# Mixture-of-experts down-projection turned to tokens on the partitions, in a fused two-layer attention kernel

## The reference

```python
logits = jnp.einsum('bsd,de->bse', x, Wg)          # x: layer-normed, E = 8 experts
top_vals, top_idx = jax.lax.top_k(logits, 2)
probs = jax.nn.softmax(top_vals, axis=-1)
weights = jnp.einsum('bsk,bske->bse', probs, jax.nn.one_hot(top_idx, 8))
for e in range(8):
    u = jnp.einsum('bsd,dh->bsh', x, W1[e])        # D = 128, H = 256
    v = jnp.einsum('bsd,dh->bsh', x, W2[e])
    h = u * jax.nn.sigmoid(u) * v
    y = jnp.einsum('bsh,hd->bsd', h, W3[e])
    out = out + y * weights[..., e][..., None]
...
Q = (decoder_input @ W_q); K = (encoder_output @ W_k)   # next block, 16 heads of 8
```

## Time and profile before

| | |
|---|---|
| time, median of 3 runs | 232.7 us (232.6 to 235.12) |
| profiled execution, its own time | 232.4 us |
| its span, first to last instruction | 230.6 us |
| PE matmul busy | 191.9 us, 83% |
| PE weight load busy | 146.3 us, 63% |
| DVE busy | 167.3 us, 73% |
| ACT busy | 138.5 us, 60% |
| POOL busy | 121.5 us, 53% |
| mean granted TensorE clock | 0.947 of full |

### The profile page before, as it was taken

The page is one execution under the profiler, slowest core; times in us unless marked ns, Lnnn a source line. Parts: engine busy times, 40 slices in busy tenths (PEclk is TensorE's granted clock), DMA queues, the critical chain, the costliest instruction groups (busy, mean ns, idle before and its releaser), DMA issues.

```text
span 230.6 us, 4033 instructions
## 1 busy us (share of the span) xinstructions
PE 191.9 (83%) x1182; PEld 146.3 (63%) x1182; DVE 167.3 (73%) x408; ACT 138.5 (60%) x273; POOL 121.5 (53%) x140
## 2 busy tenths in 40 slices
PE   5858884887989999999989689799999999886320
PEld 4646772556767888788877477566867776654220
DVE  3775774187797787699764896798978978735664
ACT  2182845965535656456652569887968769573452
POOL 4368548994867998859991452222313222203512
PEclk9999998599999999999999889999999999999755
DMA  6990000001911420207400000000000000000002
GB/s 237 395 386 9 4 0 0 0 0 44 280 45 20 167 85 9 91 0 239 126 3 1 0 0 3 0 0 4 0 4 0 0 0 0 4 0 0 0 1 91
DMA packets 6292, 12.98 MB, mean 56 GB/s; under 512 B 1009, under 2 KB 1906, under 8 KB 6018
## 3 DMA queue, kind: packets, MB, share of 16 engines
q1 hardware_dynamic: 4688, 11.83, 15.1%
q10 hardware_dynamic: 1586, 0.93, 1.4%
HBM read 10.11 MB, written 0.56 MB: 46 GB/s over the span
## 4 chain that ended last, share of the span: by engine, by line
PE 54%; POOL 14%; DVE 13%; ACT 10%; issue 8%; DVEq 0%; POOLq 0%; ACTq 0%
POOL hids L308 7%; PE banks L1344 6%; PE bank L1325 6%; PE bank L1356 5%; PE bank L1097 4%; PE bank L1098 4%; PE bank L1099 4%; PE banks L1097 3%; PE banks L1099 3%; PE banks L1098 3%; POOL cpT L318 3%; PE bank L1111 2%; PE bank L1333 2%; PE bank L1271 2%; ACT raw L593 2%
## 5 line engine op out<-in xcount | busy, mean ns | idle before, releaser
L308 POOL TENSOR_TENSOR hids<-attT,hids 128x512 fp32r<-128x512 f32 x32 | 41.1, 1300 | 10.5 <-ACT hids L509 10.1
L965 DVE TENSOR_REDUCE negm<-bank 128x2 f32<-128x512 f32 x64 | 42.0, 687 | 5.3 <-PE bank L1325 4.0
L356 POOL TENSOR_TENSOR wx<-raw,const 32x256 fp32r<-32x256 f32 x32 | 19.5, 609 | 44.9 <-DVE raw L955 36.3
L593 ACT ACTIVATE raw<-banks 128x1024 f32<-128x1024 f32 x32 | 32.5, 1022 | 3.2 <-PE banks L1344 2.9
L509 ACT CAST hids<-attT 128x512 fp32r<-128x512 f32 x32 | 19.9, 621 | 18.8 <-DVE attT L886 10.7
L881 DVE SCALAR_TENSOR_TENSOR att<-att,bank 128x512 f32<-128x512 f32 x32 | 21.9, 684 | 12.5 <-ACT att L503 12.5
L1325 PE MATMUL bank<-wx 128*128 128x512 f32 x64 | 25.5, 440 | 1.6 <-DVE wx L975 1.5
L503 ACT ACTIVATE att<-bank 128x512 f32<-128x512 f32 x32 | 18.8, 595 | 9.4 <-PE banks L1099 7.7
L1097 PE MATMUL bank<-xT,wx 128*128 128x512 f32 x48 | 19.9, 415 | 0.8 <-DVE att L881 0.7
L1098 PE MATMUL bank<-xT,wx 128*128 128x512 f32 x48 | 19.2, 400 | 0.0
L1344 PE MATMUL banks<-wx 128*128 128x256 f32 x128 | 19.1, 293 | 0.0
(11 more groups left out here) (222 smaller groups left out, 462.9 us busy)
## 6 DMA issues: line engine op xcount, KB each, us to landing
rwb<-routing SPq DMA_DIRECT2D x8, 512.0 KB, 4.1
raw<-in_w SPq DMA_DIRECT2D x1, 2048.0 KB, 10.6
wx<-negm SPq DMA_DIRECT2D x1, 2048.0 KB, 8.7
raw<-in_w SPq DMA_DIRECT2D x1, 1024.0 KB, 10.1
xs<-in_x SPq DMA_DIRECT2D x2, 256.0 KB, 3.2
ctxT<-in_ctxT SPq DMA_DIRECT2D x1, 512.0 KB, 4.4
ctx<-in_ctx SPq DMA_DIRECT2D x1, 512.0 KB, 5.8
wl<-in_wl SPq DMA_DIRECT2D x1, 256.0 KB, 6.4
```

The source lines that it names most:

```text
L308: pool.tensor_tensor(hids[:, p, 1, k, :], hid[:, p, k, :], plain(hids[:, p, 0, k, :]), ALU.subtract).then_inc(S["hid_lo"], 1)
L593: act.activation(probs[:, g % 2, 2 * r:2 * r + 2, :, :].rearrange("p h k q -> p (h k q)"), pair[r][:, :], ACT.Exp, scale=ATT_SCALE).then_i ...
L965: dve.tensor_reduce(negm[:, g % 2, r // 2, c0:c0 + QUAD + 1:QUAD], bk[1 + r % 2][:, :].rearrange("p (h k) -> p h k", h=2), AX.X, ALU.max, ...
```

## The change

- `down` swaps its operands: `hids` is stationary, 128 tokens at a time, and W3 streams with 128 columns. Three products by two blocks by four token tiles make 24 matmuls instead of 6. The result has tokens on the partitions.
- `weigh` is four DVE instructions of 128 columns that multiply by `rw[:, tile, e]`, a value per partition, and add into `xs`. `accumulate`, the transposes of sum and weights, the store and broadcast of weights, and `add_experts` go.
- `gates` uses Silu instead of tanh, so `hidden` is one DVE instruction for a block instead of two. Two dummy activations put the loads of ACT's function table ahead of the first Silu and the next Exp. The router's softmax is a tanh.
- Routing is cut in `leaders` and the rest, a unit later. On PE `up(0)` goes ahead of `logits(0)`, and `up(1)` is issued in halves around `logits_turned(0)`.
- POOL makes the rest of `ctxTs` and `wqk` later; group 0 is projected ahead of `up(15)` and group 1 ahead of `down(14)`, into bank 7.

```diff
+            act.wait_ge(S["row_norm"], 1)
+            act.activation(spare[:, :], const[:, C_ZERO:C_ZERO + 1], ACT.Silu)
...
-                        act.wait_ge(S["gate_s"], HB * (n - 1) + k + 1)
-                    act.activation(tanhs[:, k, :], bk[2 * k][:, :], ACT.Tanh, scale=0.5).then_inc(S["tanh_s"], 1)
+                        act.wait_ge(S["hid_s"], HB * (n - 1) + k + 1)
+                    act.activation(silus[:, k, :], bk[2 * k][:, :], ACT.Silu).then_inc(S["silu_s"], 1)
...
+            for n in range(UNITS):
+                if n == 4:
+                    logits_out(1)
+                if n == UNITS - 1:
+                    proj_hi(0, 7)
+                gates(n, n == 0)
+                if n == 0:
+                    logits_out(0)
+                if n in (1, 5):
+                    gap_tanh(n // 5)
+                if n == UNITS - 1:
+                    act.wait_ge(S["km_zero"], 16)
+                    masked_keys(0, 0, True)
+                for k in range(HB):
+                    if n in (E + 3, E + 4):
+                        third_scaled(HB * (n - E - 3) + k)
+                    hidden_hi(n, k)
+                if n == UNITS - 3:
+                    norm_hi()
+            act.activation(spare[:, :], const[:, C_ZERO:C_ZERO + 1], ACT.Exp)
+            proj_hi(1, 7)
...
             def hidden(n):
...
-                    dve.scalar_tensor_tensor(gated[:, k, :], tanhs[:, k, :], 1.0, bk[2 * k][:, :],
-                                             ALU.add, ALU.mult).then_inc(S["gate_s"], 1)
-                    dve.wait_ge(S["gate_s"], HB * n + k + 1)
+                    dve.wait_ge(S["silu_s"], HB * n + k + 1)
...
-                    dve.tensor_tensor(hid[:, p, k, :], gated[:, k, :], bk[2 * k + 1][:, :], ALU.mult)\
+                    dve.tensor_tensor(hid[:, p, k, :], silus[:, k, :], bk[2 * k + 1][:, :], ALU.mult)\
...
             def weigh(n):
...
-                dve.tensor_tensor(out, bk[4 + n % 2][:, :], rwb[:, e, :], ALU.mult).then_inc(S["y_w"], 1)
+                dve.wait_ge(S["route_s"], 9 * (h + 1))
+                if e > 0:
+                    dve.wait_ge(S["y_w"], n)
+                for t in range(TPH):
+                    tile = h * TPH + t
+                    ins = dve.scalar_tensor_tensor(xs[:, tile, :], bk[4 + n % 2][:, t * P:(t + 1) * P],
+                                                   rw[:, tile, e:e + 1], xs[:, tile, :], ALU.mult, ALU.add)
+                ins.then_inc(S["y_w"], 1)
...
+            for n in range(UNITS):
+                if n == UNITS - 1:
+                    stack_keys(0, 0, True, 7)
+                    stack_queries(0, 0, True, 7)
+                hidden(n)
+                if n in (0, 4):
+                    leaders(n // 4)
+                if n in (1, 5):
+                    routing(n // 5)
...
+                if n >= 2:
+                    weigh(n - 2)
...
+            stack_keys(1, 1, True, 7)
+            stack_queries(1, 1, True, 7)
             weigh(UNITS - 2)
...
             maxima(0, 0, range(2), True)
-            stack_queries(1, 1, True)
-            stack_keys(1, 1, True)
+            weigh(UNITS - 1)
             maxima(0, 0, range(2, 4), True)
...
             def down(n):
...
-                for k in range(HB):
-                    ins = three(bk[4 + p][:, :], (w3[:, e, 0, k * P:(k + 1) * P], w3[:, e, 1, k * P:(k + 1) * P]),
-                                (hids[:, p, 0, k, :], hids[:, p, 1, k, :]), k == 0, k == HB - 1)
+                for t in range(TPH):
+                    rows = slice(t * P, (t + 1) * P)
+                    for k in range(HB):
+                        cols = slice(k * P, (k + 1) * P)
+                        pe.matmul(bk[4 + p][:, rows], hids[:, p, 0, k, rows], w3[:, e, 0, cols],
+                                  start=t == 0 and k == 0, stop=False)
+                        pe.matmul(bk[4 + p][:, rows], hids[:, p, 0, k, rows], w3[:, e, 1, cols], start=False, stop=False)
+                        ins = pe.matmul(bk[4 + p][:, rows], hids[:, p, 1, k, rows], w3[:, e, 0, cols],
+                                        start=False, stop=t == TPH - 1 and k == HB - 1)
...
+            up(0)
+            pe.wait_ge(S["v_ev"], 2)
+            logits(0)
+            up(1, (0,))
+            logits_turned(0)
+            up(1, (1,))
...
+                if n == UNITS - 1:
...
+                    for a in range(2):
+                        project(0, 0, 0, a, bank=7)
+                up(n)
+                if n == 4:
+                    logits_turned(1)
+                down(n - 2)
+                if n == 3:
+                    logits(1)
+                if n == UNITS - 3:
+                    turn("ln3", "x3T_ps", 6, 0)
+            for a in range(2):
+                project(1, 1, 0, a, bank=7)
             down(UNITS - 2)
...
+            pe.wait_ge(S["hid_s"], HB * UNITS)
             for r in range(2):
                 scores(0, 0, r, True)
+            down(UNITS - 1)
             for a in range(2):
-                project(1, 1, 0, a)
+                project(2, 2, 0, a)
```

More of the change, by code:

```diff
@@ L181, in build @@
               for i in range(8)]
+        leader = bk[7][:, 64:64 + TPH]
+        topf, shares = (bk[7][:, c0:c0 + 2 * TPH].rearrange("p (t r) -> p t r", r=2) for c0 in (72, 80))
+        second = bk[7][:, P:P + TPH * E].rearrange("p (t e) -> p t e", t=TPH)
         names = """
@@ L833, in _, with leaders @@
                     .then_inc(S["xT_lo"], 1)
-            def routing(h):
+            def leaders(h):
                 tiles = slice(*HALVES[h])
@@ L1004, in dve_batch @@
                         stack_keys(m + 2, (g + 2) % G, first and g < 2)
-                    if first and g == 0:
-                        add_experts(1)
                     if more:
@@ L1269, in second_half_part @@
-            def second_half_part(src, first=False, last=False):
-                for t in range(TPH):
-                    ins = pe.matmul(bk[7][:, t * P:(t + 1) * P], src[:, t * P:(t + 1) * P], ident,
-                                    start=first and t == 0, stop=last and t == TPH - 1)
-                if last:
-                    ins.then_inc(S["accT_ps"], 1)
-            pe.wait_ge(S["xT_lo"], 1)
-            pe.wait_ge(S["v_ev"], 2)
-            logits(0)
-            up(0)
-            logits_turned(0)
@@ L1281, in _ @@
-            up(1)
-            weights_turned(0)
-            for n in range(2, UNITS):
-                up(n)
-                down(n - 2)
-                if n == 2:
-                    pe.wait_ge(S["xT_lo"], 2)
-                    logits(1)
-                if n == 3:
-                    logits_turned(1)
-                if n == 4:
-                    weights_turned(1)
-                if n == UNITS - 6:
-                    first_half_turned()
-            def project(m, g, b, a, late=None, early=False):
-                if a == 0 and not early:
+                for t in range(TPH):
[7 more added lines that the diff above has]
+                                        start=False, stop=t == TPH - 1 and k == HB - 1)
@@ L1299, in project @@
+                ins.then_inc(S["y_ps"], 1)
+            def project(m, g, b, a, late=None, bank=0):
+                if a == 0:
                     pe.wait_ge(S["ks_s"], m)
@@ L1387, in pe_batch @@
                     turn_maxima(m, g)
-                    if first and g == 2:
-                        pe.wait_ge(S["moe_s"], 2)
                     if first and g == 3:
```

273 lines of the change are left out of this document (81 added, 192 removed).

## The result

| | before | changed |
|---|---|---|
| median of the runs beside each other | 233.5 us | 243.39 us |
| profiled execution, its own time | 232.4 us | 243.39 us |
| span | 230.6 us | 241.5 us |
| mean granted clock | 0.947 | 0.93 |

The changed kernel is slower: ratio 1.042, 95% interval 1.035 to 1.049. One of its four executions was disturbed (1092.92 us) and is left out here (with it the median is 244.21); the others took 243.36 to 245.03. In a second comparison the same two kernels gave 241.65 (241.44 to 241.95) and 234.59 us, ratio 1.0319 (1.0236 to 1.0402). The forecast, 241.2 us and 237 to 246, holds both.

A forecast was written before the change was run, and what follows sets the result against it. PE's matmul pace was taken as the bound: +20.8 us for matmuls, 11.7 given back by routing wait, transposes and early projections, 0.6 by DVE, so +8.5 us and 241.2 us, range 237 to 246.

The forecast's parts named there:

- The pace of the new matmuls: Down-projection on PE: each 128-column matmul costs its load, 0.112 us; a `down` takes 2.69 us instead of 1.39, +20.8 us over 16.
- The rival with hidden loads: The 384 matmuls of `down`: 0.058 us each if only streaming counts, total 220.5 us; chance 0.05.
- the one in which load and stream follow each other: Matmuls of `down`: load does not overlap the short matmul ahead, 0.163 us each, +19.6 us, total 260.8; chance 0.03.
- DVE, ACT, POOL: Expert units: DVE 2.4 to 2.5 us, POOL 2.6, all below half of 5.47 us, so savings are worth nothing there.
- The start: Start of expert block: 0.2 us wait for the first Silu, PE reaches `up(2)` at 50.9 us instead of 53.66.
- To the second pair of maxima: From `up(2)` to the anchor, DVE's `maxima` of group 1: 138.9 us against 129.79, +9.1 us.
- The cover under ACT's load: Change into attention: ACT loads Exp's table and rounds group 1 before `down(14)` ends, with 1.1 us of cover left.
- the third rival: Change into attention comes later than summed, costing another 1.5 to 4 us, total 242.7 to 245.2; chance 0.14.
- Behind the anchor: After group 1's `maxima`, DVE does one 0.6 us instruction less (`add_experts`) before `shifted`: -0.6 us.
- Rival 4: PE's clock: a tenth of the `up` matmuls run at half clock, +4 us, total 245; chance of the loss 0.04.
- the converse: Transition near 131.0 us: denser work may lose the clock's fall to 1.2 GHz, worth under 1 us since DVE bounds there.
- the 2.13 us given back: First units of the expert block: PE's 2.13 us wait for routing of half 0 goes, falling in slack of units 1 and 2.

## Why the prediction was right

**The pace of the new matmuls**, forecast 0.112 us from one-column and fp32 rows, measured 0.111: right, and for the reason given, since the load alone sets it (the pair of runs with 32 columns). 24 of them take 2.66 us (2.69 forecast), a unit 5.43 (5.47). The pace at which the change would win, 0.090 us, was never near. The rival with hidden loads is out, and so is the one in which load and stream follow each other: that needs 0.163 us. By the Trainium skill ("TensorE: Matmul & The Clock Gate", section "Back-to-back issue gap") the time would have been 229.3 us at 81 ns; this trace's 0.111 us decides against that figure for fp32r.

**DVE, ACT, POOL.** `weigh` was put at 1.1 us and took 1.12; two `hidden` of 0.68 and one `weigh` are 2.48 us a unit, as forecast, and PE waits for none of it between 53.12 and 134.7 us. DVE was to be below half; in the window shown, which holds other work of DVE too, it is at 6.04 of 10.85 us.

**The start.** 0.35 us of wait for the first Silu, 0.2 forecast. `up(2)` came at 53.12 instead of 50.9; 2.16 of the 2.22 us are the later start of the block, at 1.2 GHz in code that the change doesn't touch. This term wasn't in the sum, and couldn't be read from one profile of the kernel before: it belongs to the spread of 2 us between executions. The table load took 1.28 us and ACT's next instruction stood 0.01 us behind it. The Trainium skill ("ScalarE: Activation LUTs", section "What ACT_TABLE_LOAD costs") adds a drain, 2.66 us in all; neither of the two new loads shows it ahead of, or behind, 1.28 us.

**To the second pair of maxima.** From `up(2)` to the end of `down(14)`: 82.2 us forecast, 134.77 - 53.12 = 81.65 measured. Then scores, `down(15)`, `weigh(15)` and two maxima: 5.8 forecast, 140.5 - 134.77 = 5.7 measured. The anchor moved by 140.5 - 129.79 = 10.7 us, 9.1 forecast; less the 2.16 us of clock it is 8.5, so the sum was 0.6 us too high.

**The cover under ACT's load** was put at 1.1 us, and this term was wrong: there was none. ACT's `stack` input was ready at 134.93, 0.16 us behind the end of `down(14)`. The forecast let ACT round unit 15 as soon as that was computed, but `hidden_hi(15)` overwrites what `down(13)` reads, and waits 1.39 us for it (the first of ACT's rows above). POOL's rest of unit 15 is late by the same wait: ready at 134.90, 6.2 us behind `up(15)` and not 4, and 0.4 us ahead of `down(15)`. Neither reached the sum, by little: DVE, which idled 2.25 us for ACT, had finished its two maxima at 138.06, and PE's `down(15)` let `weigh(15)` start at 138.12. So the third rival, which had 0.14, did not come true, but with 0.06 us of slack on DVE and not with 1.1; that was luck. No run took the table load out.

**Behind the anchor** -0.6 us was forecast for `add_experts`. The first `shifted_scores` of group 1 stands at 146.78 (136.71 before): +10.1 after +10.7. Right. The end is at +10.9, 0.8 us more. The last fall of the clock lies at 224.7 instead of 216.4 us, 8.3 us later where the work is 10.1 later; whether the 0.8 us are this isn't shown.

**The clock.** Rival 4 with its fall inside the experts did not occur (2.4 GHz from 47.2 to 224.7 us), and what it called the converse did: the stretch at 131 us is gone. That it should be worth "under 1 us" was not measured by itself. In other kernels a fall at this place came with more: 20 us at 1.2 GHz with the early projection undone, 6.8 us with the old operands or with 256-column streams.

**Where the forecast's reasoning had a hole:** it treated "routing in parts" as a matter of order, and the 2.13 us given back as free. With the old operands, where PE waits for `rw`, they are had only with the scratch tiles in PSUM; in SBUF the same order costs more than it gives (the pair 230.62 and 238.35 us). In the changed kernel DVE alone needs the weights and has some 3 us to spare in a unit (2.48 of 5.43), so what its tiles in PSUM are worth there isn't shown: no run puts them in SBUF.

As a whole: the operands cost 15.7 us, measured by themselves, and the other edits give back 8.7 us of it. The kernel to keep is the one with the old operands and the new routing, 230.62 us beside 233.98. The one with all edits but the operands ran at 225.93 us, but lacks the weighing that its layout needs, so that time is a bound and no version; of the 8.7 us only some 3.4 were had with the old layout.

## What to carry to other kernels

When PE is the bound, count loads of 128 stationary columns before you swap operands: each matmul costs 0.11 us here, whether it streams 32 or 128 columns, and with 256 columns it costs no more than 0.12. Look too at tiny instructions that stand beside a working POOL with all operands in SBUF, if PE waits for what they make: their place was worth 7.7 us. And price a waiting PE with the clock that follows it: having 1.4 us of projection and 1.9 us of stacking done ahead of the last `down`s was worth 6 to 8 us.

## What the runs showed of the hardware that was not expected

- A PE that is busy all the time by the profile can lose its clock: 85.00 of 85.00 us busy at a mean granted clock of 0.78, when two thirds of its matmuls stream 32 columns. With 128 columns it stayed at 1.00.
- DVE operations from SBUF to SBUF stood still beside POOL, 3.52 us for 0.3 us of work, those with an operand in PSUM did not, 0.28 us. The Trainium skill ("SBUF — State Buffer", section "🔬 SBUF: two separate sides") says that DVE and GpSimd share a pair of ports as an exclusive lock for a whole instruction, which a DVE operation with two SBUF inputs takes too, against a GpSimd operation that reads SBUF, as POOL's subtractions here do. The trace agrees: DVE went on at 61.73, when POOL's row ended at 61.76. Two TENSOR_SCALARs with one SBUF input and their output in SBUF, 1.32 us instead of 0.22, waited as well.
- The same code at the same place is granted 1.2 or 2.4 GHz in different executions, some 2 us of a kernel of 233.
